# Sparse attention with a feed-forward layer on one core: TensorE counts the marks by rank, the flags become bits of a word, and the second layer norm is applied one head later

## The reference

```
def sparsemax(x):
    x = x - max(x);  zs = sort(x, descending);  cssv = cumsum(zs) - 1
    k = max(sum(zs > cssv / rho), 1);  tau = cssv[k - 1] / k
    return clip(x - tau, 0)

x = x + xattn(layernorm(x), ctx)        # q = x Wq + bq, k = ctx Wk + bk, v = ctx Wv + bv
                                        # attn = sparsemax(q k^T / sqrt(32)); (attn v) Wo + bo
n = layernorm(x)
x = x + sqrt((n cos(theta + noise))^2 + (n sin(phi + noise))^2)
```

## Time and the profile before

| | us |
|---|---|
| median of 3 runs | 724.58 |
| lowest and highest of them | 724.3, 726.02 |
| the profiled execution | 725.45 |
| its span, first to last instruction | 723.7 |
| PE busy | 584.8 |
| DVE busy | 609.3 |
| ACT busy | 380.7 |
| POOL busy | 187.1 |

### The profile page before, as it was taken

The page is one execution under the profiler, slowest core; times in us unless marked ns, Lnnn a source line. Parts: engine busy times, 40 slices in busy tenths (PEclk is TensorE's granted clock), DMA queues, the critical chain, the costliest instruction groups (busy, mean ns, idle before and its releaser), DMA issues.

```text
span 723.7 us, 14347 instructions
## 1 busy us (share of the span) xinstructions
PE 584.8 (81%) x4560; PEld 332.5 (46%) x4560; DVE 609.3 (84%) x2964; ACT 380.7 (53%) x657; POOL 187.1 (26%) x239
## 2 busy tenths in 40 slices
PE   3785989798814998899899998990889988997575
PEld 1343545454402654565455544550445544655242
DVE  5699799977966999999999999994899999999600
ACT  3664565766611755666566646560456665563321
POOL 2511403241220240415033502351014430301301
PEclk9879978999965999999999999996899999996857
DMA  9752131202220113130303030303102111200000
GB/s 315 237 166 72 27 103 47 59 0 71 68 76 0 28 28 101 33 84 15 110 26 95 6 105 28 106 1 84 42 1 78 39 45 31 59 17 14 11 1 11
DMA packets 33471, 44.23 MB, mean 61 GB/s; under 512 B 8353, under 2 KB 26785, under 8 KB 33382
## 3 DMA queue, kind: packets, MB, share of 16 engines
q1 hardware_dynamic: 32332, 41.16, 20.0%
q10 hardware_dynamic: 1056, 2.10, 0.8%
HBM read 23.77 MB, written 1.64 MB: 35 GB/s over the span
## 4 chain that ended last, share of the span: by engine, by line
PE 64%; issue 16%; ACT 11%; DVE 4%; SPq 3%; DMA 1%; POOL 1%; POOLq 0%; DVEq 0%
PE ring L456 33%; PE ring L522 8%; PE ring L545 5%; PE ring L599 5%; PE mix_bank L570 5%; PE ring L495 4%; PE ring L507 3%; ACT qst L674 2%; ACT S L674 2%; SPq L248 2%; ACT ctx L674 1%; DMA S<-in_L_xattn_Wk 1%; SPq L252 1%; ACT v L674 1%; ACT ks L682 1%
## 5 line engine op out<-in xcount | busy, mean ns | idle before, releaser
L929 DVE MAX8 cand<-S 100x8 f32<-100x45 f32 (+1 forms) x2048 | 223.1, 188 | 0.5 <-issue 0.4
L456 PE MATMUL ring<-wv,ctx 128*121 128x512 f16 x576 | 156.7, 392 | 0.0
L456 PE MATMUL ring<-ctx,wk 128*128 128x361 f16 x768 | 136.1, 339 | 4.5 <-DVE ctx L1108 4.5
L798 ACT ACTIVATE pT<-ring 121x800 f32<-121x800 f32 x96 | 80.5, 839 | 75.2 <-PE ring L599 75.2
L674 ACT ACTIVATE S<-ring 100x722 f32<-100x722 f32 x128 | 95.2, 774 | 27.6 <-PE ring L545 27.2
L456 PEld LDWEIGHTS ring<-ctx,wk 128*128 128x128 f16 x768 | 78.9, 104 | 58.6 <-issue 14.9
L333 POOL TENSOR_TENSOR ctx<-ctx_f,ctx 128x484 f16<-128x484 f32 x42 | 50.6, 1205 | 163.8 <-ACT ctx L674 163.4
L545 PE MATMUL ring<-kst,qst 96*100 96x361 f16 x256 | 68.0, 361 | 29.4 <-ACT S L674 12.9
L456 PEld LDWEIGHTS ring<-wv,ctx 128*121 128x121 f16 x576 | 71.8, 137 | 33.4 <-issue 7.9
L599 PEld LDWEIGHTS ring<-qst,kst 99*121 99x121 f16 x768 | 61.5, 150 | 45.5 <-issue 21.7
L341 POOL TENSOR_TENSOR ks<-k_f,ks 128x361 f16<-128x361 f32 x64 | 57.2, 894 | 90.9 <-ACT k_f L686 88.2
(11 more groups left out here) (126 smaller groups left out, 727.3 us busy)
## 6 DMA issues: line engine op xcount, KB each, us to landing
kst<-ks SPq DMA_DIRECT2D x384, 45.1 KB, 1.9
ctx_f<-in_ctx SPq DMA_DIRECT2D x45, 242.0 KB, 2.9
xq<-in_x SPq DMA_DIRECT2D x8, 200.0 KB
xr<-in_x SPq DMA_DIRECT2D x8, 200.0 KB
out_y<-att SPq DMA_DIRECT2D x8, 200.0 KB
S<-in_L_xattn_Wk ACTq DMA_DIRECT2D x1, 1024.0 KB, 6.8
wq<-in_L_xattn_Wq ACTq DMA_DIRECT2D x1, 1024.0 KB, 11.3
wcos<-in_L_ffn_theta SPq DMA_DIRECT2D x1, 1024.0 KB, 10.4
```

Of the source, the lines that this page charges most:

```text
L456: last = nc.tensor.matmul(psum, lhs(c, i), w(c, j), start=(c == 0 and n == 0), stop=(c == DC - 1 and n == 2))
L798: nc.scalar.activation(pT[0:CK, u % 3, :, :], src, ACT.Relu).then_inc(two_read, 1)
L929: last = nc.vector.max(cand[:, h, 8 * n:8 * n + 8], S[0:L, HH * (i % 2) + h, cuts[n]:cuts[n + 1]])
```

## The change

Three things change.

The count. `thresholds(i)` marks all 1024 candidates with one comparison (is_ge) that writes them ordered by rank (eight blocks of 128 marks in bf16, where the inputs are ordered by head, piece, rank). The fold, the reduction and line 979 are gone. The last of the four turns now takes only steps upwards (max with 0). PE does the sum: one fp32 product of `n_over` with ones, and eight bf16 products of a rank's 128 marks each (by -1, and +1 for rank 8), into 8 x 17 sums on one partition of PSUM. This `sum_flags(i)` now stands at the end of phase i, right behind the scores of half i + 1 (and ahead of `o_of` in even phases), where before it stood in phase i + 1 between units of `k_of`. The first `maxes` of the next half waits for `flag_ready`.

The flags. DVE reduces the 8 x 17 sums from PSUM, compares with 0.5 and multiplies by powers of two, and adds the eight to one integer (`word_i`). `settle` loads that word once and tests its bits with register arithmetic: four bits, then two, then one.

The second layer norm is applied behind the eighth head in place of the seventh.

```diff
             def sum_flags(i):
                 pe.wait_ge(flag_ready, i + 1)
                 if i > 0:
                     pe.wait_ge(aT_ready, 2 * i)
-                nc.tensor.matmul(flag_ps, ones[:, :], n_over[:, :], start=True, stop=False)
-                nc.tensor.matmul(flag_ps, minus[:, :], n_now[:, :], start=False, stop=True).then_inc(flag_sum, 1)
+                nc.tensor.matmul(flag_ps[:, :, PIECES], ones[:, :], n_over[:, :], start=True, stop=True)
+                for r in range(8):
+                    last = nc.tensor.matmul(flag_ps[:, :, 0:PIECES], (one_b if r == 7 else minus_b)[:, :],
+                                            by_rank[:, r, :, :], start=(r == 0), stop=(r == 7))
+                last.then_inc(flag_sum, 1)
...
-                    if attended:
-                        sum_flags(i - 1)
...
                     weave(heads, fill, 1)
+                    if i < NH:
+                        sum_flags(i)
                     if b > 0:
                         run(o_of(b - 1), 4)
...
             def maxes(i, h):
                 dve.wait_ge(two_read, seen2(("s", i, h)))
+                if h == 0 and i > 0:
+                    dve.wait_ge(flag_ready, i)
...
-                last.then_inc(tau_ready, 1)
+                nc.vector.scalar_tensor_tensor(t, step_t[:, :], 0.0, t, ALU.max, ALU.add).then_inc(tau_ready, 1)
                 dve.wait_ge(tau_ready, i + 1)
-                marks = over[:, :, :].rearrange("p g (n r) -> p g n r", r=8)
-                counted(nc.vector.tensor_tensor(marks[:, :, :, 7:8], pieces[:, :, :, 7:8],
-                                                t4.broadcast_to([L, HH, PIECES, 1]), ALU.is_lt))
-                n = counted(nc.vector.tensor_tensor(marks[:, :, :, 0:7], pieces[:, :, :, 0:7],
-                                                    t4.broadcast_to([L, HH, PIECES, 7]), ALU.is_ge))
-                after(n)
-                n = counted(nc.vector.tensor_tensor(fold[:, :, 2:2 + NCAND // 2], over[:, :, 0:NCAND // 2],
-                                                    over[:, :, NCAND // 2:NCAND], ALU.add))
-                after(n)
-                n = counted(nc.vector.reduce_sum(n_now[:, :], fold[:, :, :], AX))
-                after(n)
-                nc.vector.scalar_tensor_tensor(n_now[:, :], n_now[:, :], -float(PIECES), n_over[:, :],
-                                               ALU.add, ALU.min).then_inc(flag_ready, 1)
+                nc.vector.tensor_tensor(by_rank.rearrange("p r g n -> p g n r"), pieces, t4.broadcast_to([L, HH, PIECES, 8]), ALU.is_ge).then_inc(flag_ready, 1)
...
-            def rank_flags(i):
+            def read_flags(i):
                 dve.sem_clear(check_step)
                 dve.wait_ge(flag_sum, i + 1)
-                nc.vector.scalar_tensor_tensor(code[:, :], flag_ps, 0.5, order_c[:, :],
+                nc.vector.reduce_sum(lost[:, :], flag_ps, AX).then_inc(check_step, 1)
+                dve.wait_ge(check_step, 1)
+                nc.vector.scalar_tensor_tensor(code[:, :], lost[:, :], 0.5, bit_c[:, :],
                                                ALU.is_gt, ALU.mult).then_inc(check_step, 1)
-                dve.wait_ge(check_step, 1)
-                nc.vector.max(ranked[:, :], code[:, :]).then_inc(check_step, 1)
                 dve.wait_ge(check_step, 2)
-                nc.vector.tensor_copy(ranked_i[:, :], ranked[:, :]).then_inc(check_step, 1)
+                    nc.vector.reduce_sum(word_i[:, :], code[:, :], AX).then_inc(check_step, 1)
             def settle(i):
                 dve.wait_ge(check_step, 3)
-                first = dve.value_load(ranked_i[0:1, 0:1], min_val=0, max_val=HH)
+                word = dve.value_load(word_i[0:1, 0:1], min_val=0, max_val=2 ** HH - 1)
...
-                    with dve.Fori(0, HH // 2) as pair:
-                        leading = dve.value_load(ranked_i[0:1, bass.ds(2 * pair, 1)], min_val=0, max_val=HH)
-                        with dve.If(leading > 0):
-                            with dve.Fori(0, 2) as k:
-                                number = dve.value_load(ranked_i[0:1, bass.ds(2 * pair + k, 1)], min_val=0, max_val=HH)
-                                with dve.If(number > 0):
-                                    refine(i, number)
+                    with dve.Fori(0, 2) as four:
+                        with dve.If(((word >> (4 * four)) & 15) > 0):
+                            with dve.Fori(0, 2) as pair:
+                                with dve.If(((word >> (4 * four + 2 * pair)) & 3) > 0):
+                                    with dve.Fori(0, 2) as k:
+                                        with dve.If(((word >> (4 * four + 2 * pair + k)) & 1) > 0):
+                                            refine(i, 4 * four + 2 * pair + k)
...
-                    if h == 6 and odd and b >= 1:
+                    if h == 7 and odd and b >= 1:
                         ln2_apply(b - 1)
```

More of the change, by code:

```diff
@@ L148, in build_kernel @@
         dif, over = sb("dif", [L, HH, NCAND]), sb("over", [L, HH, NCAND], BF16)
-        fold = sb("fold", [L, HH, 2 + NCAND // 2], BF16)
+        fold = sb("fold", [L, HH, 2 + PIECES * max(RANKS) // 2], BF16)
         tau = sb("tau", [L, 2, HH])
-        f_sum, step_t, n_over, n_now = (sb(n, [L, HH]) for n in ("f_sum", "step_t", "n_over", "n_now"))
-        zero, minus = sb("zero", [L, 1]), sb("minus", [L, 1])
-        order_c, code, ranked = (sb(n, [1, HH]) for n in ("order_c", "code", "ranked"))
-        ranked_i = sb("ranked_i", [1, HH], I32)
+        f_sum, step_t, n_over = (sb(n, [L, HH]) for n in ("f_sum", "step_t", "n_over"))
+        zero = sb("zero", [L, 1])
+        one_b, minus_b = sb("one_b", [L, 1], BF16), sb("minus_b", [L, 1], BF16)
+        bit_c, code, lost = (sb(n, [1, HH]) for n in ("bit_c", "code", "lost"))
+        word_i = sb("word_i", [1, 1], I32)
         again, againT = sb("again", [P, 32]), sb("againT", [P, 32])
@@ L164, in build_kernel @@
         mask_row = over[:, :, :].rearrange("p g n -> p (g n)")[:, 0:N]
+        by_rank = over[:, :, :].rearrange("p g n -> p (g n)").rearrange("p (r g n) -> p r g n", r=8, g=HH)
         s_flat = S[:, :, :].rearrange("p h n -> p (h n)")
@@ L1012, in test_sums, with refine @@
                 dve.wait_ge(fix, 3 + P // 32)
-            def refine(i, number):
-                number = nc.s_assert_within(number, 1, HH, skip_runtime_bounds_check_because="inside If(number > 0)")
-                t = tau[:, i % 2, bass.ds(number - 1, 1)]
-                row = S[0:L, bass.ds(number - 1 + HH * (i % 2), 1), :].rearrange("p a n -> p (a n)")
+            def refine(i, h):
+                h = nc.s_assert_within(h, 0, HH - 1, skip_runtime_bounds_check_because="a sum of three bits")
+                t = tau[:, i % 2, bass.ds(h, 1)]
+                row = S[0:L, bass.ds(h + HH * (i % 2), 1), :].rearrange("p a n -> p (a n)")
                 dve.sem_clear(fix)
@@ L1052, in rank_flags @@
                                                ALU.is_gt, ALU.mult).then_inc(check_step, 1)
-                dve.wait_ge(check_step, 1)
-                nc.vector.max(ranked[:, :], code[:, :]).then_inc(check_step, 1)
                 dve.wait_ge(check_step, 2)
-                nc.vector.tensor_copy(ranked_i[:, :], ranked[:, :]).then_inc(check_step, 1)
+                with nc.allow_low_precision(reason="a sum of distinct powers of two under 256"):
+                    nc.vector.reduce_sum(word_i[:, :], code[:, :], AX).then_inc(check_step, 1)
@@ L1141, in _ @@
                     if h == 3 and i > 0:
-                        rank_flags(i - 1)
+                        read_flags(i - 1)
                     if h == 4 and i > 0:
@@ L1155, in _ @@
                     ln1_apply(b + 1)
-            rank_flags(NH - 1)
+            read_flags(NH - 1)
             settle(NH - 1)
```

19 lines of the change are left out of this document (10 added, 9 removed).

## The result

| | before | after |
|---|---|---|
| median, us | 724.44 (4 runs) | 741.32 (4 runs) |
| lowest and highest | 722.93, 726.02 | 737.63, 742.12 |
| profiled execution | 725.45 | 742.12 |
| its span | 723.7 | 740.3 |

The ratio of the medians is 1.022, its 95% interval 1.018 to 1.026. The forecast was 716.0, its range 708 to 723, and "slower" had a chance of 0.08. The kernel lost 16.9 us instead of gaining 8.5.

What follows compares the result with a forecast made beforehand. PE and ACT's answers set the middle's pace; DVE sets the time at three PE waits. First refinement -5.4, second -6.8, end -1.4, PE +4.8 and +0.3: -8.5 from 725.45 gives 716.95, median 716 us; range 708 to 723.

Steps and rivals of the forecast that it cites:

- slower: Rival, in both refinements: nested tests cost more than the loads, giving 725 to 730 us; chance 0.08.
- A gain on DVE counts where its chain ends in one of these waits: PE's waits of 26.53 and 18.69 us for `verified` and 5.34 at the end: there DVE sets the time.
- -1.8 and -1.8 for the norm: Phases 3 and 9, before the refinements: the eighth head's 16 maxima move ahead of the root wait, 1.8 us each.
- -0.7 and -1.4 for the tails: Marks before the refinements: a 2.5 us tail replaces 3.18, 0.7 less each; one in the first, two in the second.
- +0.2 and +0.4 for reading the flags: Reducing 136 sums from PSUM: net 0.2 us more each time, one read in the first refinement, two in the second.
- 2.1 ns x 1024 + 0.2 = 2.4 us: DVE's one scattered comparison, priced by line 969's start-to-start figure: 2.4 us.
- the gain is eaten: Rival: comparison takes 4.7 us, four on the chain, +9.2, 725 us; or tests give nothing, 723. Together 0.15.
- Just enough; 0.3 us for the phase right behind a refinement: PE's new wait for `flag_ready`: marks come at 402.65, PE finishes its scores at 403.16; 0.3 us added.
- The tests: -7.1: Bit tests in `settle`: -1.0, -0.3 and -1.8 us in the first refinement, -1.1 and -2.9 in the second.
- PE's products: +0.44 a phase: New fp32 and eight bf16 products on PE: net +0.44 us a phase, counted in eleven phases, total +4.8.
- The end: -1.4: Phase 15: the later norm gives 1.8 us less 0.4 by PE's own work; the marks there give nothing.

Runs made afterwards that it cites:

- d: The kernel before with only the second layer norm applied behind the eighth head: 724.21 us against 724.99, ratio 0.999.
- a: The kernel after with its comparison written in input order, so PE reads every eighth mark: 754.22 us against 724.99 for the kernel before, 1.038.
- b: The kernel after with its comparison writing contiguously by rank and reading every eighth word: 731.35 us against 724.99 for the kernel before, 1.006.
- n: The kernel after, scattered comparison kept, with its nine products back at the old place between units of `k_of`: 730.11 us against 725.44 for the kernel before, 1.006.
- m: The kernel after with comparison reading every eighth word, writing contiguously, and the nine products back at the old place: 721.95 us against 724.39 for the kernel before, 0.996.
- f: The kernel before with only the flags as bits of a word, tested in registers: 720.19 us against 724.39, 0.993.
- c: The kernel after with the descending numbers and register loads of the kernel before in place of bits: 748.0 us against 724.99 for the kernel before, 1.032.

## Why the prediction was wrong, step by step

**"A gain on DVE counts where its chain ends in one of these waits": this failed.** I took the wait that ended last to be for DVE alone, since `verified` comes from DVE. DVE itself waits inside `settle` for POOL's split, and POOL for PE. The wait stands in the code (`dve.wait_ge(tau_split, i + 1)`), and my description of `settle` left it out. In the second refinement of the kernel before the split's last instruction starts at 488.89 and the sweep at 491.29, with the numbers cast since 487.57: the row's 2.02 us of idle time "<-issue" held that wait. In the first DVE was the later one, by about 0.9 us and no more, so even there a gain of 1.8 could not have arrived whole. The sum's -1.8 and -1.8 for the norm and -0.7 and -1.4 for the tails in front of the refinements bought nothing (d: 0.8, within its interval; a, b and after: the same waits to 0.02). The +0.2 and +0.4 for reading the flags cost nothing for the same reason.

**"2.1 ns x 1024 + 0.2 = 2.4 us": the price of the comparison failed,** by a factor of two. The measured price is 4.77 us. Line 971 starts 0.35 us after line 969 because DVE's instructions overlap, not because the writes ran at 2.1 ns; the busy time, 4.5 ns an element, was the price. The Trainium skill ("Vector Engine (DVE) Microarchitecture Reference", section 5.2 "Measured stream behaviour on trn2") has at most 2.51 ns a column for a hopping destination, measured with 4-byte elements; measured are 4.66 here for 2-byte marks 256 bytes apart. For reads hopping at every element its 1.73 (one source, 4 KiB hops) agrees fairly with b's 2.0 (one source, every eighth word). The rival "the gain is eaten" had the price right (4.7 us, four of them on the chain, +9.2), and nearly the effect: six on the chain instead of four, 10.0 and 8.2 us measured (after to b, n to m). It ended at 725 because it left the rest of the sum standing.

**"Just enough; 0.3 us for the phase right behind a refinement": the new place was mis-sized,** and it is 7.2 us with the old marks, 9.4 to 11.2 with the new. I checked one wait in one phase (marks at 402.65 against PE at 403.16) and did not follow what stands behind PE's wait in even phases: `o_of`, and behind it the root for which DVE waits. The loop's round, 76.1 against 75.0, could be worked out from rows of the kernel before. In the kernel after, the steady middle does escape it: marks through at 411.8, sums at 412.8, because from the root at 355.18 DVE needs 56.6 us there: 1.8 of maxima fall out of the round with the late norm, and some 3.6 because four kinds of its instructions are shorter than in the same stretch before (the subtractions of 512 elements, for one, 0.69 us instead of 1.17 on average), which together is more than the two comparisons add. That they are shorter because they no longer meet POOL's (last section) is not shown. But behind the refinement, at the start and in the last three phases DVE has no slack, and there it bit.

**The tests: -7.1, measured -4.2 (f) and -6.7 (c to after).** Right in sign and kind; the two long waits show 4.4 and 4.5. The skips of empty numbers were worth more than forecast, the way to a flagged head got dearer. The rival "slower" had the sign of the result, but by nested tests that cost more than the loads, and that is not what happened.

**PE's products: +0.44 a phase, measured +0.43.** But I left out the phases in front of the long waits. Since these waits have a fixed length behind PE's own progress, they hide nothing of PE's: all but the last phase count, 15 x 0.43 = 6.5 in place of 4.8. No run has the nine products as its only change. The phases at full clock give 0.44 each (35.31 to 35.75), and the other parts (place +7.2, comparison +8 to +10, bits -4.2, norm -0.8) leave some 5 to 7 of the 16.9; as the parts act on each other, that is no more than a check.

**The end: -1.4, measured +1.8** (7.12 us of wait against 5.34). In b it is 2.16, 5.0 less: the last two comparisons lie on the chain that ends there, and each is 2.7 us cheaper in b.

**TensorE's clock was not in the sum at all.** An estimate of what it costs is length times (1 - clock): summed over phases 2 to 14 without the two long waits it is about 16 us before and 27 after, 24 in b and 16 in m. By it some 10 of the 16.9 us are clock, in phases 3 and 11 above all. It is part of what the other items cost, not an addition to them, and of the place's above all: one phase of b is 2.8 us longer than in m. What exactly makes it fall stays open. The runs show that it changes with where small blocks and waits lie, and within one kernel it varies from run to run (b 726.1 to 732.8, m 715.5 to 724.5), so none of the terms above is known to better than about 2 us.

The reason for the sign of the result: the change bought time on DVE ahead of a wait that DVE did not end, and paid with a longer instruction and an earlier demand for its result where DVE was the one waited for.

## What to carry to other kernels

Before a gain is credited to a wait, read every semaphore that the waited-for engine itself still waits for: an idle time in front of its next instruction that says "issue" can hide a second gate, and a quick test is to delay or hasten that engine and see whether the wait changes. When a consumer is moved closer to its producer, work out the closed round through whatever stands behind the consumer, root to marks to products to root, and compare it with the present period; slack that one phase shows is not slack of the round. When data must change its order between engines, price all three ways, scattered writes, scattered reads and strided use: here 4.77, 2.05 and 1.22 us on DVE, the last with 1.34 more on PE.

## What was not expected of the hardware

- 1024 marks of 2 bytes written 256 bytes apart take 4.77 us, in order 1.22; the same permutation on the side of the reads (4-byte words, every eighth) takes 2.05.
- A moving operand of PE that takes every eighth bf16 column: eight products of 128 columns in 1.9 us, contiguous in 0.56.
- DVE and POOL disturb each other. POOL's timeline of the kernel after during the comparison of 254.52 to 259.25:

```profile
254.54 5.13 POOL L336 TENSOR_TENSOR ctx<-ctx_f,ctx 128x484 f16<-128x484 f32 x1 [3.55 <-ACT ctx L681]
```

  One conversion takes 5.13 us there, where the same one takes 1.10 in b (251.55). The other way, DVE's 16 subtractions of 512 elements take 0.69 us each in the kernel after. Before, ten of them take 0.69 and six 1.45 to 1.66, each of the six beginning just behind the start of an instruction of POOL (350.08 behind 350.03, for one). The group in the kernel after:

```profile
L953 DVE TENSOR_TENSOR dif<-cand,tau 100x512 f32<-100x512 f32 x16 | 11.1, 691 | 0.5
```

  So a shift of a few microseconds between two engines changes durations that one would take as fixed. That POOL's work is the cause is read from the coincidence; no run took it away.
- Phase 7 takes 38.6 us at a granted clock of 1.00 (after) and 41.4 at 0.92 (b), with the same products.
